# One pool of five PSUM banks, taken by a planner's account, for attention and the state-space model

## The reference

```python
h = layernorm(x) * (1 + ca) + sa ;  xn = ln(h, ln1_w, ln1_b)
# attention: 16 heads of 8, causal
q, k, v = xn @ q_w + q_b, xn @ k_w + k_b, xn @ v_w + v_b
attn_out = softmax(mask(q k^T / sqrt(8))) @ v @ o_w + o_b
# state-space model, 256 channels x 16 states
x_ssm, z = split(xn @ in_proj_w) ;  x_c = silu(causal_conv4(x_ssm) + conv_b)
dt = softplus(x_dbc[:8] @ dt_w + dt_b) ;  Bm, Cm = x_dbc[8:24], x_dbc[24:40]
h_t = exp(dt_t * A) * h_(t-1) + (x_t * dt_t) * B_t ;  y_t = sum_n C_t[n] * h_t[n]
ssm_out = ((y + x_c * D) * silu(z)) @ ssm_out_w
x = x + alpha * attn_out + (1 - alpha) * ssm_out
```

## Time and profile before

| | us |
|---|---|
| median of 3 runs (1873.93 to 1879.81) | 1875.94 |
| the profiled execution's own time | 1875.14 |
| its span, first to last instruction | 1873.3 |
| mixer stage with both streams in it, read off the timeline | about 116 to 1040 |
| end of attention alone | about 1040 to 1080 |
| everything behind | about 1080 to 1873 |

### The profile page before, as it was taken

One profiled execution on the slowest core, in us unless ns is written; L12 is line 12 of the kernel. 1 busy time (PEld: TensorE's weight loads), 2 busy tenths in 40 slices (PEclk: granted clock), 3 DMA queues, 4 the chain that ended last, 5 costly groups with the idle time before them and its releaser, 6 DMA issues. The chain is left out here.

```text
span 1873.3 us, 22056 instructions
## 1 busy us (share of the span) xinstructions
PE 1506.9 (80%) x7196; PEld 935.3 (50%) x7196; DVE 1345.0 (72%) x2025; ACT 1066.2 (57%) x1776; POOL 846.7 (45%) x866
## 2 busy tenths in 40 slices
PE   4757777777777868777776788979999999988778
PEld 3334433434344344343443355558778787844673
DVE  2377868868778687786889167577868686848866
ACT  2555555555555554655555467567787878832107
POOL 3263646656555465554665431112222222336853
PEclk8877898988979989889899989889999999966889
DMA  3121212102122021121210021001111111100001
GB/s 80 51 71 46 65 44 71 57 28 76 54 65 64 27 70 55 45 69 40 67 62 18 1 90 52 24 17 43 45 40 45 40 45 40 51 1 1 1 1 45
DMA packets 61654, 84.72 MB, mean 45 GB/s; under 512 B 6588, under 2 KB 32038, under 8 KB 61542
## 3 DMA queue, kind: packets, MB, share of 16 engines
q1 hardware_dynamic: 61442, 83.30, 14.7%
q10 hardware_dynamic: 100, 0.03, 0.0%
HBM read 74.38 MB, written 8.78 MB: 44 GB/s over the span
## 5 line engine op out<-in xcount | busy, mean ns | idle before, releaser
L1002 PE MATMUL bank<-QK 127*128 127x128 bf16 (+7 forms) x1024 | 252.3, 331 | 126.1 <-DVE Mx L1268 115.1
L1710 POOL TENSOR_TENSOR dBx<-dtx,Bb 128x512 f32<-128x512 f32 x256 | 320.2, 1274 | 5.8 <-DVE hy L1284 5.8
L1317 DVE TENSOR_TENSOR hl<-lsq,hh 128x512 fp32r<-128x512 f32 x320 | 260.9, 826 | 84.2 <-ACT hh L1594 76.2
L1531 ACT ACTIVATE PT<-bank 128x512 f32<-128x512 f32 x320 | 188.2, 595 | 204.8 <-PE bank L1002 203.9
L1284 DVE TENSOR_TENSOR_SCAN hy<-bank,dBx 128x512 f32<-128x512 f32 x256 | 298.1, 1205 | 4.7 <-POOL dBx L1710 4.3
L1268 DVE TENSOR_REDUCE Mx<-bank 128x1 f32<-128x384 f32 (+3 forms) x352 | 217.6, 630 | 88.9 <-PE bank L1002 88.3
L1591 ACT ACTIVATE lsq<-bank,vcol 128x512 f32<-128x512 f32 x320 | 219.1, 693 | 108.0 <-DVE hl L1317 63.2
L1690 POOL TENSOR_SCALAR_AFFINE_SELECT PT<-PT 128x256 f32<-128x256 f32 (+1 forms) x320 | 118.2, 375 | 302.6 <-ACT PT L1531 301.2
L1729 POOL TENSOR_TENSOR stage<-stage,lrs 128x512 f32<-128x512 f32 x64 | 91.7, 1433 | 311.2 <-DVE lrs L1397 311.2
L1002 PEld LDWEIGHTS bank<-QK 127*128 127x128 bf16 (+1 forms) x1024 | 94.3, 106 | 273.3 <-DVE Mx L1268 178.8
L1002 PE MATMUL bank<-x,we1h 128*128 128x512 f32 x640 | 210.8, 411 | 18.8 <-DVE x L1305 9.4
(11 more groups left out here) (255 smaller groups left out, 2475.3 us busy)
## 6 DMA issues: line engine op xcount, KB each, us to landing
Bb<-b_dram SPq DMA_DIRECT2D x128, 256.0 KB, 3.7
stage<-w_rows SPq DMA_DIRECT2D x64, 256.0 KB, 3.2
parts<-part SPq DMA_DIRECT2D x16, 384.0 KB, 2.8
QK<-parts SPq DMA_DIRECT2D x64, 96.0 KB
QK<-parts SPq DMA_DIRECT2D x64, 64.0 KB
stage<-in_L_ffn_We_dram SPq DMA_DIRECT2D x16, 256.0 KB, 3.4
hy<-in_L_attn_x_dram SPq DMA_DIRECT2D x8, 256.0 KB, 5.6
QK<-parts SPq DMA_DIRECT2D x64, 32.0 KB
```

Source lines behind the costliest of these rows:

```text
L1002: return engine.matmul(o, l, r, start=start, stop=stop, tile_position=pos, skip_group_check=True)
L1317: engine.tensor_tensor(hl[:, sl, :], full[:, f, :], hh[:, sl, :].bitcast(F32), ALU.subtract).then_inc(sems["dve_hl"], 1)
L1531: engine.activation(PT[:, it["sl"], :], o[:], ACT.Exp).then_inc(sems["act_exp"], 1)
L1710: engine.tensor_tensor(dBx[:, sl, h], dtx[:, b % 2, h], Bb[:, sl], ALU.mult).then_inc(sems["pool_dbx"], 1)
```

## The change

Three parts. First, the planner keeps a rough account of the engines' work: each event that a step announces costs what a table `WORK` says (in units of 10 ns, 60 where the table has no entry; 300 for a DMA), starts when the step's named events are over, and moves on the account of its engine. Second, one list of five banks, 0, 1, 2, 6 and 7, takes the place of the two round robins, and each take chooses the bank that by the account is free first; among those that the account holds free before PE gets there, it takes the one picked longest ago. Steps with two banks (`dbc`, `taps`) choose both at once. Third, while the first norms run, which use banks 0 to 5 themselves, the list is only 6 and 7.

No instruction is added, removed or moved on any engine; what changes is which bank a step writes, and so which event its PE instruction waits for. The account exists only while the program is built.

```diff
+WORK = dict(pe_max=45, pe_sc=30, pe_ht=45, pe_av=200, pe_qk=95, pe_val=95, pe_mrow=45, pe_dn=95, pe_wo=190, pe_bx=350, pe_dbc=180, pe_dt=95,
+            pe_yt=45, pe_so=190, pe_lnc=95, pe_lnv=95, dve_max=62, dve_scan=113, dve_y=40, dve_ha=70, dve_hs=70, dve_yd=70, dve_qk=50,
+            dve_lno=70, dve_lns=40, dve_bc=20, act_exp=55, act_da=61, act_y=80, pool_dbx=125, pool_sel=40, act_silu=240)
 class Plan:
     def __init__(self):
...
+        self.load = dict(pe=0, dve=0, act=0, pool=0)
+        self.when, self.now = {}, 0
     def up(self, sem, by=1):
         self.count[sem] += by
+        engine = sem.split("_")[0]
+        if engine in self.load:
+            self.last[engine] = (sem, self.count[sem])
+            self.now = self.load[engine] = max(self.load[engine], self.now) + by * WORK.get(sem, 60)
+        else:
+            self.now += 300
+        self.when[sem, self.count[sem]] = self.now
         return (sem, self.count[sem])
+    def at(self, x):
+        if not isinstance(x, (tuple, list)):
+            return 0
+        if len(x) == 2 and isinstance(x[0], str):
+            return self.when.get(x, 0)
+        return max(map(self.at, x), default=0)
+    def first_free(self, banks):
+        k = min(banks, key=lambda x: max(self.at(self.free.get(f"b{x}")), self.load["pe"]))
+        banks.remove(k)
+        banks.append(k)
+        return k
     def step(self, kind, /, **fields):
         self.steps.append((kind, fields))
+        self.now = max(map(self.at, fields.values()), default=0)
         return fields
...
-    ring, ring2 = [0, 1, 2], [0]
+    ring = [0, 1, 2, 6, 7]
...
     def take():
-        ring.append(ring.pop(0))
-        return ring[-1]
-    def take2():
-        ring2[0] += 1
-        return 6 + (ring2[0] - 1) % 2
+        return p.first_free(ring)
+    def take_two():
+        k = p.first_free(ring)
+        ring.remove(k)
+        k2 = p.first_free(ring)
+        ring.append(k)
+        return k, k2
...
-            k = take2()
+            k = take()
...
-        k, k2 = take2(), take2()
+        k, k2 = take_two()
...
+    ring[:] = [6, 7]
     run_together(p.norms(first_norms([(1, 1)] + [(b, l) for l in range(2) for b in range(2, NB)])), 12, (mixer, 5, False))
+    ring[:] = [0, 1, 2, 6, 7]
```

More of the change, by code:

```diff
@@ L48, in __init__ @@
         self.last = {}
+        self.load = dict(pe=0, dve=0, act=0, pool=0)
+        self.when, self.now = {}, 0
     def up(self, sem, by=1):
         self.count[sem] += by
-        if sem.split("_")[0] in ("pe", "dve", "act", "pool"):
-            self.last[sem.split("_")[0]] = (sem, self.count[sem])
-        return (sem, self.count[sem])
+        engine = sem.split("_")[0]
[5 more added lines that the diff above has]
+        self.when[sem, self.count[sem]] = self.now
+        return (sem, self.count[sem])
+    def at(self, x):
[9 more added lines that the diff above has]
+        return k
     def step(self, kind, /, **fields):
         self.steps.append((kind, fields))
+        self.now = max(map(self.at, fields.values()), default=0)
         return fields
```

## The result

| | before | changed |
|---|---|---|
| median, same job | 1874.93 us (1872.59 to 1879.81) | 1718.7 us (1717.36 to 1719.02) |
| ratio | | 0.916, 95% interval 0.914 to 0.918 |
| the same again, another job | 1873.52 | 1719.05, ratio 0.917 (0.915 to 0.919) |
| span of the profiled execution | 1873.3 | 1716.3 |

The account below looks back on a forecast made before the run. Neither PE nor DVE was held to bound the mixer stage; they wait for each other. Of 105 us on the path 75 were taken: 1875.14 - 75 = 1800, forecast 1801 us; range 1758 to 1870.

Parts of the forecast that it names:

- stalls for a bank: Mixer stage, PE steps taking a bank: 189 of 208 us of stalls avoidable; longest-ago order alone would leave 37 us.
- well under 100: Sign of being right: PE's waits on L1268 and hy L1206 fall from 202 us to well under 100 us.
- a selection too rough: Account's prices partly wrong, such as `weigh` at 2.0 against 1.07: no cost added, part of the gain missed, within the 75.
- slower rival: Mixer stage: shared banks let attention and state-space tiles block each other, 55 us added, about 1930 us; chance 0.12.
- point of decision: Mixer stage: slower from 87 picks of a bank behind a pair of scans, 208 / 2.4, one in 13 takes.
- the sign of failing this way: Prediction fails downward if DVE's idle time before hT and bc, put down to long PE work, goes as well.
- PE's bursts: Mixer stage: long PE work giving DVE nothing (`weigh`, `on` with `wo`, `bx`), held mainly behind 87 us of DVE gaps.
- What of it lies on the path: Mixer stage: 105 of 192 us of DVE's idle gaps covered by avoidable PE stalls, 62 of them before maxima.
- What comes back: Mixer stage: denser DVE frees banks later, PE fills all five and stalls again; 75 of the 105 us taken.
- the 194 us that I excluded as a bound: Mixer stage: gain if DVE were never idle, 924 - 730 = 194 us; excluded because PE's long work stays.
- the rival built on it: Mixer stage: short waits bring PE's granted clock from 0.88 to 0.77, gain only 9 us, 1866 us; chance 0.04.
- rival "more": Mixer stage: the full 105 us and a little of the other 87, below 1775, about 1765 us; chance 0.08.

Follow-up runs that it names:

- short `bx`: Kernel before with one of the four products of each `bx` (three convolution taps left out), 43 us less PE work: ratio 0.996 (0.993 to 1.000).
- measured prices: Changed kernel with the account's prices set to what the trace shows (`weigh` 1.05 for 2.0, `bz` 1.12 for 3.5, POOL's operations): 1718.3 us, ratio 0.921.
- lumps: Four products of each `bx` done twice, 57 us more PE work in 16 pieces: 1773.2 us in the changed kernel, 1922.2 us in the kernel before.

## Why the prediction was right or wrong

Right: the stage, the engines, the direction, and nothing outside it that the change did (-150 in the stage, 0 in the tail, -7 behind it where the clock was higher). Right that the stalls for a bank were avoidable (PE's waits on L1268 and hy went from 202 to 83 us, "well under 100") and that sharing alone, without a working account, would take most of them away (124 of some 150 us). Right that a selection too rough costs only a part; the account is worth 23 to 30 us. The slower rival's mechanism exists, 54 us of PE's waits without the account, and falls far short of its point of decision.

Wrong in size, in two terms of the sum: 105 - 30 = 75 us of DVE's idle time were to go, and 144 went (cut alike, 190 us before and 46 now). Only this net is measured; how it divides between the two terms is read from the waits. The prediction had named the sign of failing this way, that idle time before hT and bc, "put down to PE's bursts, goes as well", and it went.

*What of it lies on the path: 105 us, where 144 went.* The waits of DVE by cause, predicted to go / gone: before maxima 62 / 74, before bc 13 / 35, before hy 16 / 22, before hT 12 / 16. I had credited a gap to a stall of PE only if the stall had ended within 6 us before the gap's end, and called the other 87 us bursts. The worst miss is bc: no PE instruction of `dbc` or before it changed, and the wait went from 5.3 us a time to nearly none; it stayed with split banks and was 22.6 us with four shared ones, so it hung on how many banks `dbc` could choose its two from, and hardly on a burst (with the short `bx` 31.4 of its 37.1 us were left). Shortening `bx` in the kernel before moved the time by 5 us in 43, which shows that its bursts alone did not make the gaps: what PE saved it waited off at banks. A stall delays all that PE does until it next catches up, and the 6 us cut that memory off; that this, and not something else, explains the rest of the difference is my reading, no run isolates it.

*What comes back: 30 us, where none shows.* No cause in the list above gave less than was predicted. I took back 30 of the 105 us because PE would fill five banks and stall again. It does, for 77 us on maxima and some 25 on the other groups for a bank shown, but a stall of PE costs no time while DVE still has tiles in hand: 56 us of PE work more, spread, cost 2 to 6. The stall by itself is no sign of that, since PE waited 150 us on maxima in the kernel before too, with DVE idle for 190; what tells the two apart is whether DVE is idle soon after. The bound on the gain should have been DVE's work plus the gaps that no bank can close: the cast behind ACT, 15.9, and the first scan behind POOL, 4.3, so 724 + 20 = 744 us for the stage. With the 22 us that the changed kernel shows before maxima and hT, known only now, it is 766; 764 was measured. And of the 194 us that I excluded as a bound three quarters came true.

*The clock.* I priced only a fall. It rose, from 0.88 to 0.96 in the stage, and PE's same work took 619 us instead of 689 (682 when cut alike). In the changed kernel this is off the path: with the measured prices the stretch between the scans was as short at 0.92. What the low clock cost the kernel before was not measured. The Trainium skill (TensorE: Matmul & The Clock Gate, "A second HAM failure mode: psum-queue depth-cycling") puts the swings of the clock in a kernel that cycles through PSUM banks down to brief pauses of PE between groups of matmuls. Here a cycle of more banks left PE idle for 19% of the stage in place of 25%, and the clock was higher, 0.96; the cycling as such did not bring it down, and the rival built on it did not come.

The rival "more" had the right mechanism at 0.08, and its time of 1765 was still 46 us too high. With the idle time at what it measured the sum is 1875.14 - 144 = 1731; DVE's busy time, 6 us less in the stage, and the 7 us behind it lead to 1718, where the profiled execution took 1718.54.

## What to carry to other kernels

In this kernel two engines handed tiles to each other and both were idle for a fifth to a quarter of the time. The time to expect once they share enough buffers was the fuller engine's work plus the gaps that no buffer can close, with nothing taken back for stalls of the emptier engine. Enough matters: with four shared banks DVE was still idle for 91 us of the stage, with five for 46. Streams that share an in-order producer should share its buffers as well: sharing gave twice what a clever choice inside split buffers gave. The choice was worth having on top, with prices that tell a long operation from a short one; making them more exact gained nothing. Test slack by adding work, once spread and once in lumps; they answer different questions, and only the lumps find the places where the cover is used up. And cut two traces at the same instruction, not at a round time, before setting stage against stage.

## What the runs showed of the hardware

The granted clock could be moved without touching what PE computes. Over the whole kernel and all runs it was 0.893 to 0.911 in the kernel before, 0.908 to 0.918 with split banks and the account, 0.923 to 0.929 with four shared banks, 0.926 to 0.936 with five in fixed order, and 0.934 to 0.942 in the changed kernel; in the mixer stage of the profiled executions it was 0.88, 0.92, 0.93, 0.94 and 0.96. It is not fixed by the kernel: with the measured prices one run had 0.914 and three had 0.937 to 0.940, at 1723.9 us against 1716 to 1718, and the stretch between the scans of the 0.914 run was as short as any. In one job the 13 runs of the kernel before went from 1859 us at 0.909 to 1876 at 0.895, which is part of why it times less evenly than the changed kernel.

The 512 extra transposes raised the clock of the kernel before to 0.912 to 0.928, where that kernel itself had 0.893 to 0.906 in the same job. So 56 us of PE work at full clock made PE's busy time in the stage only 36 us longer and the kernel 10 us slower. In the changed kernel the same transposes gave 0.940 to 0.950, hardly more than without them.
